# Gated cross-attention and a mixture of experts: token-major rows loaded first, one unbroken warming, and routing moved by one batch

## The chip, the cores and the metric

The kernel runs on one core of a Trainium2 chip. A core has a matmul engine (TensorE, PE in the profile), a vector engine (VectorE, DVE), an activation engine (ScalarE, ACT), a general engine (GpSimd, POOL) and a queue engine (SyncE, SP); each runs its own list of instructions in order, and they meet at semaphores. The metric is the device time of one execution in microseconds (us), lower is better.

## What is computed

Eight batches of 112 tokens with 256 values each, a context of 375 rows for each batch, and eight experts.

```python
def _L0_xattn_ref(x, w1, w2):                 # w1 = w2 = ctx_1024, one context per batch
    h = jnp.einsum('eth,efh->etf', x, w1)
    g = jax.nn.gelu(h, approximate=True)
    return jnp.einsum('etf,efh->eth', g, w2)

def _L0_ffn_ref(x, gate_w, gate_b, w1, b1, w2, b2):
    logits = xf @ gate_w.T + gate_b           # xf: all 896 tokens
    top1 = jnp.argmax(logits, axis=-1)
    ...
    h = jax.nn.relu(xf @ w1[e].T + b1[e])     # for each expert e of 8
    y = h @ w2[e].T + b2[e]
    out = out + jnp.where((top1 == e)[:, None], y, ...)

x = x + jnp.tanh(g_xattn[0]) * _L0_xattn_ref(_layernorm(x), ctx_1024, ctx_1024)
x = x + jnp.tanh(g_ffn[0]) * _L0_ffn_ref(_layernorm(x), gate_w, gate_b, w1, b1, w2, b2)
```

## The kernel before, in words

The program has two halves. The first is the attention, batch by batch (b = 0 to 7). The second sends each token only to its own expert: tokens are sorted into blocks of 128 rows by expert, gathered from DRAM, and each block passes through its expert.

**Loads.** SyncE issues all loads in one queue, in the order of its code (L237 to L261): the rows of batch 0 and of batch 1, the transposed contexts (`cxT`, 375 KB each) of batches 0 and 1, the rows of batches 2 and 3, those of 4 to 7, then the plain context rows (`cx`) and the other contexts, then weights. After the weights of expert 1 and the first half of expert 2 it waits until the gathered rows of the first blocks have landed (L255 to L258), and loads the rest.

**Attention.** For a batch, VectorE takes mean and variance (`stats_x`, L508 and L510), GpSimd makes 1/std (`of_x`, L305 and L308), VectorE normalises (`norm_x`, L514), TensorE transposes (`turn_xn`, L855) and ScalarE copies (`xnT_copy`, L414). TensorE then computes `scores` (L865) and the gate logits of x (`x_logits`, L874; VectorE scales them in L519), ScalarE applies gelu (L422), and TensorE applies `attend` (L883). VectorE adds the result to x (`add_attention`, L525), takes the statistics of the new rows (L532, L536), GpSimd makes their 1/std (`of_x2`), and ScalarE stores the rows to DRAM (`store_x2`, L430). TensorE runs `scores(b + 1)` ahead of `attend(b)`. Before the first rows are there it multiplies an identity matrix by itself (`keep_warm`, L962): 4, 4, 2 and 1 times, between other steps.

**Routing.** `route` on VectorE (L553 to L572) finds the expert of each token of a batch. `rank_sums` on TensorE (L890 to L899, small bf16 matmuls) counts the tokens of the same expert that stand before each token; `own_count` and `rank_of` (L600, L605), or `rank_one` (L609) for one batch, read the count out on VectorE. `pick` on GpSimd (L320) turns a rank into a 0/1 matrix. From the picks of batches 0 to 2 TensorE makes the first block of expert 0 without a gather (`first_block`, L920, after ScalarE's L436); from all of them it makes the table of rows (`tokens`, L926), for which it also needs `place` (L326). The order in which GpSimd takes these steps is written by hand:

```python
            for b in range(B - 1):
                of_x2(b)
                if b == 4:
                    for c in range(EARLY):
                        pick(c, 1)
            for b in range(3, 6):
                pick(b, 2)
            of_x2(B - 1)
            place()
            pick(6, 3)
```

**Experts.** TensorE runs `up` (L946; 32 matmul records for a block) and `down` (L955; 16 records), with `turn_block` (L933) between, for nine blocks; `up(0, (0,))` and `up(0, (1,))` are two eighths of the first, which stand among the rank sums. ScalarE and VectorE apply bias and relu (L464, L754), VectorE finishes a block (L770), GpSimd gathers blocks (L344) and scatters results (L349).

Of the kernel before, what the change touches and what calls it, by code (L numbers as in the profile page):

```python
# [19 lines left out]
P = 128  # L20
# [19 lines left out]
RAW = X0 + D  # L40
SL = S + E
CHUNKS = TOKENS // P
WARM = 4
AHEAD = 4
EARLY = 3
BLOCKS = E + 1
# [7 lines left out]
def gated_cross_attention_moe(nc, x, ctx, small, w1t, w2t, b2, out):  # L54
    x2_dram = nc.dram_tensor("x2_rows", (TOKENS, ROW), F32, kind="Internal").ap()
    with ExitStack() as stack:
# [6 lines left out]
        def sem(name):  # L63
            return stack.enter_context(nc.semaphore(name))
# [101 lines left out]
        y_over_ps = banks[7]  # L166

        def ranks(b):
            return {B - 2: banks[1], B - 1: banks[6]}.get(b, rk_ps)


        x_in = [sem("x_in0"), sem("x_in1"), sem("x_in2"), sem("x_in4")]
        small_in, b2_in = sem("small_in"), sem("b2_in")
        cxT_in = [sem("cxT_in0"), sem("cxT_in1"), sem("cxT_in2")]
        cx_in = [sem(f"cx_in{b}") for b in range(B)]
# [43 lines left out]
        @block.sync  # L219
        def _(sp):  # L220
            def load_context(b):
                sp.dma_start(cxs[:, b, :], ctx[b]).then_inc(cx_in[b], 16)

            def load_context_T(b):
                sp.dma_start(cxT[:, b, :], ctx[b, :, 0:KD * CTX]).then_inc(cxT_in[b], 16)

            def load_context_rows(b):
                sp.dma_start(cx[:, b, :], ctx[b, :, KD * CTX:CW]).then_inc(cx_in[b], 16)

            def load_expert(e):  # L230
                sp.dma_start(w1[:, e, :], w1t[e]).then_inc(w1_in[e], 16)
                sp.dma_start(w2[:, e, :], w2t[e]).then_inc(w2_in[e], 16)

            def load_x(b, n):
                return sp.dma_start(x2[0:S, b:b + n, X0:RAW], x[b * S:(b + n) * S].rearrange("(b p) d -> p b d", p=S))  # L235

            load_x(0, 1).then_inc(x_in[0], 16)  # L237
            load_x(1, 1).then_inc(x_in[1], 16)
            load_context_T(0)
            load_context_T(1)  # L240
            load_x(2, 2).then_inc(x_in[2], 16)
            load_x(4, 4).then_inc(x_in[3], 16)
            load_context_rows(0)
            load_context_T(2)
            load_context_rows(1)
            load_context_rows(2)
            for b in range(3, B):
                load_context(b)

            load_expert(0)  # L250
            sp.dma_start(b2b[:], b2.partition_broadcast(P)).then_inc(b2_in, 16)
            load_expert(1)
            sp.dma_start(w1[:, 2, :], w1t[2]).then_inc(w1_in[2], 16)

            sp.wait_ge(xnT_done, B)  # L255
            sp.wait_ge(xgT_done, 1)
            sp.wait_ge(first_in[1], 16)
            sp.wait_ge(xg_in[0], 16)  # L258
            sp.dma_start(w2[:, 2, :], w2t[2]).then_inc(w2_in[2], 16)
            for e in range(3, E):  # L260
                load_expert(e)  # L261

        @block.gpsimd
        def _(pool):
# [49 lines left out]
            def of_x2(b):  # L314
                pool.wait_ge(stats2_ok, b + 1)
                inverse_std(x2[0:S, b, MEAN:X0]).then_inc(rstd2_ok, 1)

            def pick(b, group):
                pool.wait_ge(rank_ok, group)
                pool.tensor_scalar(pick_r0[0:S, b, :], iota_r[0:S, :], rank[0:S, b:b + 1], None,  # L320
                                   ALU.is_equal).then_inc(picks0_ok, 1)
# [6 lines left out]

            for b in range(B):
                of_x(b)  # L330
            for b in range(B - 1):
                of_x2(b)
                if b == 4:
                    for c in range(EARLY):
                        pick(c, 1)
            for b in range(3, 6):
                pick(b, 2)
            of_x2(B - 1)
            place()
            pick(6, 3)  # L340


            def gather(to, idx):
                return pool.indirect_dma_start(  # L344
# [157 lines left out]
        @block.vector  # L502
        def _(dve):
            def stats_x(b):
                dve.wait_ge(x_in[b if b < 2 else 2 + b // 4], 16)
                if b >= 1:
                    dve.wait_ge(stats_ok, b)
                dve.bn_stats(stats[0:S, :], x2[0:S, b, X0:RAW]).then_inc(s1_ok, 1)  # L508
                dve.wait_ge(s1_ok, b + 1)
                dve.bn_aggr(mv[0:S, b, 0:2], stats[0:S, :]).then_inc(stats_ok, 1)  # L510

            def norm_x(b):
                dve.wait_ge(rstd_ok, b + 1)
                dve.tensor_scalar(xn[0:S, b, :], x2[0:S, b, X0:RAW], mv[0:S, b, 0:1], mv[0:S, b, 2:3],  # L514
                                  ALU.subtract, ALU.mult).then_inc(xn_ok, 1)

            def x_logits(b):
                dve.wait_ge(lg_done, b + 1)
# [78 lines left out]

            def own_count(b, n, group):
                dve.wait_ge(rk_done, group)
                dve.tensor_tensor(rk[0:S, b:b + n], rk_ps[0:S, b * E:(b + n) * E].rearrange("p (b e) -> p b e", b=n),  # L600
                                  oh[0:S, b:b + n], ALU.mult).then_inc(rank_read, 1)

            def rank_of(b, n, group):
                dve.wait_ge(rank_read, group)
                dve.tensor_reduce(rank[0:S, b:b + n], rk[0:S, b:b + n], AX_X, ALU.add).then_inc(rank_ok, 1)  # L605
# [10 lines left out]
                                  idw[0:S, B - 1, :].unsqueeze(2).to_broadcast([S, 2, E]), ALU.mult).then_inc(place_last_ok, 1)  # L616

            def pick_last():
                dve.wait_ge(rank_ok, 4)
                dve.tensor_scalar(pick_r0[0:S, B - 1, :], iota_r[0:S, :], rank[0:S, B - 1:B], None,  # L620
                                  ALU.is_equal).then_inc(pick_last_ok, 1)

            stats_x(0)
            stats_x(1)
            dve.wait_ge(gm_done, 1)
            for q in range(2):
                dve.tensor_tensor(xnT[:, q, :].rearrange("p (k n) -> p k n", k=KD)[:, :, S:SL],
                                  gw.rearrange("p (k e) -> p k e", k=KD),
                                  gm_ps[:, 0:E].unsqueeze(1).to_broadcast([P, KD, E]), ALU.subtract).then_inc(gwc_ok, 1)
            norm_x(0)  # L630
            norm_x(1)
            for b in range(2, 6):
                stats_x(b)
            norm_x(2)
            norm_x(3)
            dve.wait_ge(tg_ok, 1)
            dve.wait_ge(consts_ok, 11)
            x_logits(0)
            stats_x(6)
            stats_x(7)  # L640
            norm_x(4)
            norm_x(5)

            for b in range(B):
                add_attention(b)
                stats_x2(b)
                join_x2(b)
                if b + 1 < B:
                    x_logits(b + 1)
                if b == 0:  # L650
                    norm_x(6)
                    norm_x(7)
                if 1 <= b <= EARLY:
                    norm_x2(b - 1)
                if b == 3:
                    route(0, 3, 1)
                    is_expert_0()
                if b == 4:
                    skip_room()
                    own_count(0, 3, 1)  # L660
                    rank_of(0, 3, 1)
                    route(3, 1, 2)
                if b == 5:
                    route(4, 1, 3)
                if b == 6:
                    route(5, 1, 4)
            route(6, 1, 5)
            own_count(3, 3, 2)
            rank_of(3, 3, 2)
            route(7, 1, 6)  # L670
            place_last()
            rank_one(6, 3)
            rank_one(7, 4)
            pick_last()

            dve.wait_ge(tok0_done, 1)
# [172 lines left out]
        def _(pe):  # L849
# [58 lines left out]
                mm.then_inc(rk_done, 1)  # L908

            def rank_sums_before_last():  # L910
                for back in range(1, B):
                    batches_before(B - 1, 1, back, start=(back == 1), stop=False)
                past_room(B - 1, 1)
# [49 lines left out]

            pe.wait_ge(ident_ok, 1)
            keep_warm(WARM)
            pe.wait_ge(gmean_ok, 1)
            pe.wait_ge(small_in, 16)
            for k in range(KD):
                mm = pe.matmul(gm_ps[:, 0:E], g_mean[:], gw[:, k * E:(k + 1) * E], start=(k == 0), stop=(k == KD - 1))
            mm.then_inc(gm_done, 1)  # L970
            keep_warm(4)
            turn_xn(0)
            keep_warm(2)
            turn_xn(1)
            keep_warm(1)
            pe.wait_ge(gwc_ok, 2)
            scores(0)
            x_logits(0)
# [1 line left out]
            for b in range(B):  # L980
                if b + 1 < B:
                    scores(b + 1)
                    x_logits(b + 1)
                if b + 2 < B:
                    turn_xn(b + 2)
                attend(b)
                if b == 4:
                    pe.wait_ge(consts_ok, 11)
                    pe.wait_ge(oh_ok, 1)
                    for c in range(EARLY):  # L990
                        pe.matmul(rk_ps[0:1, B * E:(B + 1) * E], ones[0:S, 0:1], oh[0:S, c, :], start=(c == 0),
                                  stop=(c == EARLY - 1))
                    rank_sums(0, 3)

            for b in range(EARLY):
                pe.wait_ge(pick_x_ok, b + 1)
                mm = first_block(b)
            mm.then_inc(xgT_done, 1)
            pe.wait_ge(oh_ok, 4)
            rank_sums(3, 3)  # L1000
            up(0, (0,))
            pe.wait_ge(oh_ok, 5)
            rank_sums(6, 1)
# [136 lines left out]
```

## Time and profile before

| | us |
|---|---|
| median of 3 runs | 121.02 (119.59 to 121.82) |
| the profiled execution | 120.62 |
| its span | 118.8 |
| TensorE busy | 107.0 |
| VectorE busy | 54.5 |
| GpSimd busy | 37.4 |
| ScalarE busy | 27.2 |
| mean granted TensorE clock | 0.958 of full |

The span is the part of the execution between the first and the last instruction of the engines; the profiled execution took 1.8 us more than that. TensorE is busy for nine tenths of the span, so the stretches that matter are those in which it is idle or its granted clock is low. "Busy" says nothing of how fast the work goes: a matmul at half the clock is as busy as one at full clock.

### The profile page before, as it was taken

The page shows a single profiled execution, that of the slowest core. Times are in us where ns is not written, and L with a number is a line of the kernel's source. Part 1 is how long each engine was busy: PE and PEld are TensorE (multiplying, and loading weights), DVE is VectorE, ACT ScalarE, POOL GpSimd, SP SyncE. Part 2 cuts the span into 40 slices and gives each one's busy share as a digit, 9 for nine tenths or more (in the row PEclk, how much of TensorE's full clock was granted, in tenths as well). Part 3 has the DMA queues.
Part 4 walks back from the last instruction along what each step waited for, and adds up shares of the span by engine and source line. Part 5 has one row for each costly group of instructions (what it writes and reads, how often), then busy time and mean ns, then how long its engine had stood idle before and what let it go on. Part 6 is the DMA issues. An engine that isn't in the chain of part 4 may idle for free.

```text
span 118.8 us, 2178 instructions
## 1 busy us (share of the span) xinstructions
PE 107.0 (90%) x741; PEld 98.8 (83%) x742; DVE 54.5 (46%) x210; ACT 27.2 (23%) x82; POOL 37.4 (32%) x81
## 2 busy tenths in 40 slices
PE   4999999999968938999999999999999999999900
PEld 4999799997946928999999999989999899998800
DVE  0706965579666447566465351333422243141210
ACT  5521322220313120423332230412304123030000
POOL 6705742222522454770060273302003030030330
PEclk9999999999999995599999999999999999999995
DMA  3999999999999410359999999999401000010100
GB/s 91 241 271 302 417 415 413 420 428 405 429 419 423 186 39 3 77 126 390 368 417 416 372 419 378 399 425 430 197 19 40 0 0 34 0 44 0 37 18 28
DMA packets 7037, 28.32 MB, mean 238 GB/s; under 512 B 1133, under 2 KB 2927, under 8 KB 4848
## 3 DMA queue, kind: packets, MB, share of 16 engines
q1 hardware_dynamic: 4992, 25.06, 54.2%
q0 software_dynamic: 864, 2.12, 6.1%
q10 hardware_dynamic: 1168, 0.98, 2.5%
q8 instruction: 7, 0.11, 0.4%
q14 instruction: 6, 0.05, 0.1%
HBM read 26.30 MB, written 2.11 MB: 239 GB/s over the span
## 4 chain that ended last, share of the span: by engine, by line
PE 74%; DVE 8%; DMA 6%; POOL 4%; issue 2%; SPq 2%; POOLq 0%; DVEq 0%
PE bank L946 29%; PE bank L955 26%; PE bank L883 8%; DMA x<-in_x 6%; PE bank L865 6%; POOL pick_r L320 2%; PE bank L933 1%; PE bank L874 1%; DVE x L525 1%; DVE stats L532 1%; SPq L235 1%; DVE cand L563 1%; POOL out_rows L349 1%; PE bank L855 1%; DVE lg L553 1%
## 5 line engine op out<-in xcount | busy, mean ns | idle before, releaser
L946 PE MATMUL bank<-region,w 128*128 128x128 f32 x288 | 37.1, 289 | 0.0
L946 PEld LDWEIGHTS bank<-region,w 128*128 128x128 f32 x288 | 36.2, 203 | 0.5
L955 PE MATMUL bank<-w,region 128*128 128x256 f32 x144 | 32.6, 379 | 0.0
L955 PEld LDWEIGHTS bank<-w,region 128*128 128x128 f32 x144 | 26.7, 191 | 3.2
L464 ACT ACTIVATE region<-bank,smalls 128x128 f32<-128x128 f32 x40 | 12.5, 363 | 46.4 <-PE bank L946 42.8
L349 POOL DMA_INDIRECT out_rows<-region,to_row x9 | 8.9, 989 | 36.7 <-DVE region L770 36.1
L754 DVE TENSOR_SCALAR region<-bank,smalls 128x128 f32<-128x128 f32 x32 | 9.7, 346 | 16.0 <-PE bank L946 15.4
L344 POOL DMA_INDIRECT region<-x_rows,from_row x9 | 9.3, 1031 | 15.5 <-DMA region<-x_rows,from_row 12.0
L770 DVE SCALAR_TENSOR_TENSOR region<-bank,tg,region 128x256 f32<-128x256 f32 (+1 forms) x9 | 4.3, 483 | 20.9 <-PE bank L955 20.9
L883 PE MATMUL bank<-region,w 125*112 125x264 f32 x48 | 12.2, 389 | 1.7 <-DVE x L519 1.7
L865 PEld LDWEIGHTS bank<-xnT,region 128*125 128x125 f32 x96 | 12.4, 202 | 0.4
L865 PE MATMUL bank<-xnT,region 128*125 128x120 f32 x96 | 12.7, 286 | 0.0
L883 PEld LDWEIGHTS bank<-region,w 125*112 125x112 f32 x48 | 7.8, 176 | 3.8 <-issue 2.3
L422 ACT ACTIVATE w<-bank 125x336 f32<-125x336 f32 x8 | 3.6, 450 | 16.6 <-PE bank L865 13.5
L962 PE MATMUL bank<-ident 128*128 128x128 f32 x22 | 5.9, 437 | 1.6 <-POOL ident L268 1.6
L525 DVE SCALAR_TENSOR_TENSOR x<-bank,tg,x 112x264 f32<-112x264 f32 x8 | 3.9, 491 | 6.4 <-PE bank L883 6.4
L508 DVE BATCH_NORM_STATS2 stats<-x 112x6 f32<-112x256 f32 x8 | 3.4, 426 | 6.9 <-DMA x<-in_x 6.5
L962 PEld LDWEIGHTS bank<-ident 128*128 128x128 f32 x22 | 5.1, 331 | 1.3 <-POOL ident L268 1.3
L305 POOL TENSOR_TENSOR x<-x,eps 112x1 f32<-112x1 f32 x8 | 1.5, 190 | 13.7 <-DVE x L536 13.7
L320 POOL TENSOR_SCALAR pick_r<-iota_r,rank 112x128 bf16<-112x128 bf16 x7 | 4.2, 605 | 5.0 <-DVE rank L605 3.7
L308 POOL TENSOR_TENSOR mv<-mv,power 112x1 f32<-112x1 f32 x8 | 4.6, 574 | 0.6
L441 ACT ACTIVATE region<-bank 128x256 f32<-128x256 f32 x9 | 3.5, 384 | 5.6 <-PE bank L933 4.5
(117 smaller groups left out, 88.3 us busy)
## 6 DMA issues: line engine op xcount, KB each, us to landing
w<-in_w1t SPq DMA_DIRECT2D x8, 1024.0 KB, 22.0
w<-in_w2t SPq DMA_DIRECT2D x8, 1024.0 KB, 22.2
region<-in_ctx SPq DMA_DIRECT2D x5, 771.0 KB, 13.5
region<-in_ctx SPq DMA_DIRECT2D x3, 396.0 KB, 9.0
region<-in_ctx SPq DMA_DIRECT2D x3, 375.0 KB, 5.7
b2b<-in_b SPq DMA_DIRECT2D x1, 1024.0 KB, 24.5
x_rows<-x ACTq DMA_DIRECT2D x8, 113.8 KB, 6.6
x<-in_x SPq DMA_DIRECT2D x1, 448.0 KB, 7.7
```

Of the source, the lines that this page charges most:

```text
L308: return pool.tensor_tensor(v[:, 2:3], v[:, 3:4], power[0:S, :], ALU.pow)
L320: pool.tensor_scalar(pick_r0[0:S, b, :], iota_r[0:S, :], rank[0:S, b:b + 1], None, ALU.is_equal).then_inc(picks0_ok, 1)
L344: return pool.indirect_dma_start(out=to, out_offset=None, in_=x2_dram, in_offset=bass.IndirectOffsetOnAxis(ap=idx, axis=0), bounds_check=T ...
L349: return pool.indirect_dma_start(out=out, out_offset=bass.IndirectOffsetOnAxis(ap=idx, axis=0), in_=rows, in_offset=None, bounds_check=TOK ...
L464: act.activation(hidT[:, q, 2 * k + r, :], hT_ps[k][:, r * P:(r + 1) * P], ACT.Relu, bias=b1[:, bass.ds(e * KH + 2 * k + r, 1)]).then_inc( ...
L525: dve.scalar_tensor_tensor(out=x2[0:S, b, X0:ROW + E], in0=at_ps[b % 2][0:S, 0:DL], scalar=tg[0:S, 0:1], in1=x2[0:S, b, X0:ROW + E], op0=A ...
L754: dve.tensor_scalar(hidT[:, q, 2 * k + r, :], hT_ps[k][:, r * P:(r + 1) * P], b1[:, bass.ds(e * KH + 2 * k + r, 1)], 0.0, ALU.add, ALU.max ...
L865: mm = pe.matmul(sc_ps[b % 2][0:CR, c * SL:(c + 1) * SL], cxT[:, b, k * CTX + c * CR:k * CTX + (c + 1) * CR], xnT[:, b % 2, k * SL:(k + 1) ...
L883: mm = pe.matmul(at_ps[b % 2][0:S, 0:DL], gel[0:CR, b % 2, c * S:(c + 1) * S], cx[0:CR, b, c * DL:(c + 1) * DL], start=(c == 0), stop=(c = ...
L946: mm = pe.matmul(hT_ps[k][:, part % 2 * P:(part % 2 + 1) * P], w1[:, e, n * H + part * P:n * H + (part + 1) * P], xgT[:, j % 2, n * P:(n + ...
L955: mm = pe.matmul(y[:, 0:D], hidT[:, q, part, :], w2[:, e, part * D:(part + 1) * D], start=(part == 0), stop=(part == KH - 1))
L962: pe.matmul(sc_ps[1][:, 0:P], ident[:], ident[:], start=True, stop=True)
```

## The change

Five things change. (1) x is given to the program with the token first, `(S, B, D)`, and the rows of batches 2 to 7 are one load of 6 KB for each partition, issued ahead of the contexts. (2) The warming of TensorE is nine multiplications in one stretch ahead of the first transpose, and one more ahead of the second. (3) VectorE's first steps come in another order: the rows of batches 0 and 1 are normalised before the gate weights are centred, and the statistics and normalisations of batches 5, 6 and 7 are all done before the first `add_attention`. (4) The routing steps after batch 4 move one batch later or earlier: ranks of batches 0 to 2 are read in step 5 and no longer in step 4, those of 3 and 4 form a group that is summed and read in step 6, and batch 5 is taken alone right after the loop; the sums of 3 and 4 go to another PSUM bank. (5) On GpSimd, picks are issued behind the 1/std of a later batch: 0 to 2 behind that of batch 5, 3 and 4 behind that of batch 6, and the 1/std of batch 7 no longer stands behind the pick of batch 5.

```diff
-WARM = 4
+WARM = 9
...
-            return {B - 2: banks[1], B - 1: banks[6]}.get(b, rk_ps)
+            return {EARLY: banks[6], B - 2: banks[1], B - 1: banks[6]}.get(b, rk_ps)
...
-                return sp.dma_start(x2[0:S, b:b + n, X0:RAW], x[b * S:(b + n) * S].rearrange("(b p) d -> p b d", p=S))
+                return sp.dma_start(x2[0:S, b:b + n, X0:RAW], x[:, b:b + n, :])
             load_x(0, 1).then_inc(x_in[0], 16)
             load_x(1, 1).then_inc(x_in[1], 16)
+            load_x(2, B - 2).then_inc(x_in[2], 16)
             load_context_T(0)
             load_context_T(1)
-            load_x(2, 2).then_inc(x_in[2], 16)
-            load_x(4, 4).then_inc(x_in[3], 16)
...
-            for b in range(B - 1):
+            for b in range(6):
                 of_x2(b)
-                if b == 4:
-                    for c in range(EARLY):
-                        pick(c, 1)
-            for b in range(3, 6):
+            for b in range(EARLY):
+                pick(b, 1)
+            of_x2(6)
+            for b in range(EARLY, 5):
                 pick(b, 2)
-            of_x2(B - 1)
+            of_x2(7)
+            pick(5, 3)
             place()
-            pick(6, 3)
+            pick(6, 4)
...
+            def centre_gates(q):
+                dve.wait_ge(gm_done, 1)
+                dve.tensor_tensor(xnT[:, q, :].rearrange("p (k n) -> p k n", k=KD)[:, :, S:SL],
+                                  gw.rearrange("p (k e) -> p k e", k=KD),
+                                  gm_ps[:, 0:E].unsqueeze(1).to_broadcast([P, KD, E]), ALU.subtract).then_inc(gwc_ok, 1)
...
             stats_x(0)
             stats_x(1)
-            dve.wait_ge(gm_done, 1)
-            for q in range(2):
...
             norm_x(0)
             norm_x(1)
-            for b in range(2, 6):
-                stats_x(b)
+            centre_gates(0)
+            centre_gates(1)
+            stats_x(2)
+            stats_x(3)
             norm_x(2)
+            stats_x(4)
             norm_x(3)
             dve.wait_ge(tg_ok, 1)
             dve.wait_ge(consts_ok, 11)
             x_logits(0)
-            stats_x(6)
-            stats_x(7)
-            norm_x(4)
-            norm_x(5)
+            for b in range(5, B):
+                stats_x(b)
+                norm_x(b - 1)
+            norm_x(B - 1)
...
-                if b == 0:
-                    norm_x(6)
-                    norm_x(7)
...
                 if b == 4:
+                    route(3, 1, 2)
+                if b == 5:
+                    route(4, 1, 3)
                     skip_room()
                     own_count(0, 3, 1)
                     rank_of(0, 3, 1)
-                    route(3, 1, 2)
-                if b == 5:
-                    route(4, 1, 3)
                 if b == 6:
                     route(5, 1, 4)
+                    own_count(3, 2, 2)
+                    rank_of(3, 2, 2)
+            rank_one(5, 3)
             route(6, 1, 5)
-            own_count(3, 3, 2)
-            rank_of(3, 3, 2)
             route(7, 1, 6)
             place_last()
-            rank_one(6, 3)
-            rank_one(7, 4)
+            rank_one(6, 4)
+            rank_one(7, 5)
             pick_last()
...
             def rank_sums_before_last():
+                pe.wait_ge(rank_read, 2)
...
             keep_warm(WARM)
+            turn_xn(0)
             pe.wait_ge(gmean_ok, 1)
             pe.wait_ge(small_in, 16)
...
-            keep_warm(4)
-            turn_xn(0)
-            keep_warm(2)
+            keep_warm(1)
             turn_xn(1)
-            keep_warm(1)
             pe.wait_ge(gwc_ok, 2)
...
+                if b == 6:
+                    pe.wait_ge(oh_ok, 3)
+                    rank_sums(3, 2)
+            pe.wait_ge(oh_ok, 4)
+            pe.wait_ge(rank_read, 1)
+            rank_sums(5, 1)
             for b in range(EARLY):
                 pe.wait_ge(pick_x_ok, b + 1)
                 mm = first_block(b)
             mm.then_inc(xgT_done, 1)
-            pe.wait_ge(oh_ok, 4)
-            rank_sums(3, 3)
             up(0, (0,))
             pe.wait_ge(oh_ok, 5)
             rank_sums(6, 1)
```

## Rows read from the trace of the kernel before

**Rows 1.** The page, parts 1 and 2: TensorE's share, its granted clock in 40 slices

```profile
PE 107.0 (90%) x741; PEld 98.8 (83%) x742; DVE 54.5 (46%) x210; ACT 27.2 (23%) x82; POOL 37.4 (32%) x81
...
PEclk9999999999999995599999999999999999999995
```

**Rows 2.** Busy time by stretch: PE, PEld, DVE, ACT, POOL, clock, DMA share, GB/s

```profile
42.00:44.00 2.00, 0.13 (x2) 0.00 (x0) 0.94 (x5) 0.62 (x2) 1.15 (x4) 1.00 0.10 29
44.00:46.00 2.00, 1.40 (x27) 1.28 (x28) 1.25 (x12) 0.00 (x0) 0.62 (x1) 0.52 0.10 33
...
51.00:54.00 3.00, 3.00 (x18) 2.62 (x17) 2.60 (x15) 0.65 (x3) 1.89 (x2) 1.00 0.68 192
```

**Rows 3.** The chain that ended last, 40 to 63 us: start, length, what

```profile
40.32 1.77 POOL pick_r L320 x3
...
42.32 0.58 POOL x L308
42.92 0.34 DVE lg L553
...
45.80 5.33 PE bank L946 x24
...
54.80 2.68 PE bank L946 x24
...
62.76 0.22 PE bank L933 x2
```

**Rows 4.** The timeline, 34 to 45 us: start, length, engine, line, idle before

```profile
34.69 0.49 DVE L525 SCALAR_TENSOR_TENSOR x<-bank,tg,x 112x264 f32<-112x264 f32 x1 [0.76 <-PE bank L883]
...
36.18 1.56 PE L883 MATMUL bank<-region,w 125*112 125x264 f32 x6 [1.53 <-DVE x L519]
...
37.20 0.98 ACT L436 ACTIVATE w<-pick_r,is_e 112x128 f32<-112x128 bf16 x3 [3.77 <-POOL x L308]
37.65 1.60 PE L920 MATMUL bank<-w 112*128 112x128 f32 x12
...
38.77 0.18 DVE L536 BATCH_NORM_AGGREGATE x<-stats 112x2 f32<-112x6 f32 x1
...
40.52 0.83 PE L894 MATMUL bank<-oh,ones 112*112 112x8 bf16 x13
...
41.42 0.71 PE L946 MATMUL bank<-region,w 128*128 128x128 f32 x4
...
44.16 0.25 PE L890 MATMUL bank<-oh,tri 112*112 112x8 bf16 x1 [2.03 <-DVE oh L572]
```

**Rows 5.** The timeline, 1 to 19 us

```profile
1.60 2.07 PE L962 MATMUL bank<-ident 128*128 128x128 f32 x8 [1.60 <-POOL ident L268]
...
8.23 2.30 PE L865 MATMUL bank<-xnT,region 128*125 128x120 f32 x12
...
10.87 0.43 DVE L508 BATCH_NORM_STATS2 stats<-x 112x6 f32<-112x256 f32 x1 [0.68 <-DMA x<-in_x]
...
14.29 0.70 DVE L514 TENSOR_SCALAR w<-x,mv 112x256 f32<-112x256 f32 x2
14.91 0.49 DVE L525 SCALAR_TENSOR_TENSOR x<-bank,tg,x 112x264 f32<-112x264 f32 x1
...
17.82 1.47 PE L865 MATMUL bank<-xnT,region 128*125 128x120 f32 x12
```

**Rows 6.** Issues in short windows, 2.6 to 4 us: KB each, us to landing

```profile
x<-in_x SPq DMA_DIRECT2D x1, 224.0 KB, 6.1
...
x<-in_x SPq DMA_DIRECT2D x1, 448.0 KB, 7.7
region<-in_ctx SPq DMA_DIRECT2D x1, 396.0 KB, 8.2
```

**Rows 7.** The timeline at 51 us, and that gather's time to landing

```profile
50.89 1.00 POOL L344 DMA_INDIRECT region<-x_rows,from_row  x1 [0.30 <-issue]
...
region<-x_rows,from_row POOLq DMA_INDIRECT x1, 8.2
```

More of the change, by code:

```diff
@@ L168, in ranks @@
         def ranks(b):
-            return {B - 2: banks[1], B - 1: banks[6]}.get(b, rk_ps)
-        x_in = [sem("x_in0"), sem("x_in1"), sem("x_in2"), sem("x_in4")]
+            return {EARLY: banks[6], B - 2: banks[1], B - 1: banks[6]}.get(b, rk_ps)
+        x_in = [sem("x_in0"), sem("x_in1"), sem("x_in2")]
         small_in, b2_in = sem("small_in"), sem("b2_in")
@@ L504, in stats_x @@
             def stats_x(b):
-                dve.wait_ge(x_in[b if b < 2 else 2 + b // 4], 16)
+                dve.wait_ge(x_in[min(b, 2)], 16)
                 if b >= 1:
@@ L599, in own_count @@
                 dve.wait_ge(rk_done, group)
-                dve.tensor_tensor(rk[0:S, b:b + n], rk_ps[0:S, b * E:(b + n) * E].rearrange("p (b e) -> p b e", b=n),
+                dve.tensor_tensor(rk[0:S, b:b + n], ranks(b)[0:S, b * E:(b + n) * E].rearrange("p (b e) -> p b e", b=n),
                                   oh[0:S, b:b + n], ALU.mult).then_inc(rank_read, 1)
@@ L618, in pick_last @@
             def pick_last():
-                dve.wait_ge(rank_ok, 4)
+                dve.wait_ge(rank_ok, 5)
                 dve.tensor_scalar(pick_r0[0:S, B - 1, :], iota_r[0:S, :], rank[0:S, B - 1:B], None,
@@ L624, in _ @@
             stats_x(1)
-            dve.wait_ge(gm_done, 1)
-            for q in range(2):
-                dve.tensor_tensor(xnT[:, q, :].rearrange("p (k n) -> p k n", k=KD)[:, :, S:SL],
-                                  gw.rearrange("p (k e) -> p k e", k=KD),
-                                  gm_ps[:, 0:E].unsqueeze(1).to_broadcast([P, KD, E]), ALU.subtract).then_inc(gwc_ok, 1)
             norm_x(0)
             norm_x(1)
-            for b in range(2, 6):
-                stats_x(b)
+            centre_gates(0)
+            centre_gates(1)
+            stats_x(2)
+            stats_x(3)
             norm_x(2)
+            stats_x(4)
             norm_x(3)
@@ L1116 @@
     arrays = {
-        "x": np.ascontiguousarray(x).reshape(TOKENS, D),
+        "x": np.ascontiguousarray(np.asarray(x).transpose(1, 0, 2)),
         "ctx": np.ascontiguousarray(np.concatenate([
```

## The prediction

> **What bounds the kernel now.** I read the page's slices first. TensorE is busy nine tenths of the span, and two slices at 45 to 51 us carry a granted clock of 5 tenths [rows 1]. So I asked for busy time by stretch around those slices. From 42 to 44 us TensorE does 0.13 us of work, from 44 on its clock is 0.52, and it is back at 1.00 from 51 us [rows 2]. These levels are 2.4 and 1.2 GHz. From 51 us to the end the chain of waits is TensorE alone, but for one last block's finish and scatter: whatever makes the expert phase start earlier or run faster there is worth its full length, and nothing else is.
>
> The chain names what holds TensorE at 42 to 45 us [rows 3]: three picks on GpSimd (1.77 us from 40.32), behind them the 1/std of batch 7 (0.58 from 42.32), then VectorE's route of batch 7 (from 42.92), then one more pick, then 24 matmuls of `up(0)` that take 5.33 us. The same 24 take 2.68 us at 54.80 [rows 3]. The statistics of batch 7 were ready at 38.77 + 0.18 = 38.95 [rows 4]; its 1/std stood 3.1 us behind picks which themselves waited for rank sums. That is the queue that part (5) of the change rearranges.
>
> **The change, part by part. First the routing.** I put the new order on the times of before, with the durations of before.
>
> GpSimd: the picks of 0 to 2 (1.77 us) leave 29.89 and go behind the 1/std of batch 5. VectorE reads their ranks in step 5, after `route(4)`. Those five instructions (L590 to L605) take 0.9 us, 0.18 each like L536 [rows 4]; in step 5 VectorE had 0.76 us idle ahead of its L525 at 34.69 [rows 4], so step 6 starts some 0.14 us later, and so does `attend(7)`, which waits for step 6's L519: 36.32 and not 36.18, its end 37.85. In step 4 the same 0.9 us goes away, where nothing waited for it. The picks now run from 34.85 to 36.62. The 1/std of batch 6 stands behind them: statistics ready at 36.0, start at 36.65 instead of 35.94, done 37.45. ScalarE is queued behind that with the store of batch 6 and then L436, which began at 37.20 [rows 4]; now 37.9. So `first_block` starts at 38.35 instead of 37.65 and ends at 39.95 instead of 39.25. This is a cost of 0.7 us on TensorE's path. Its cover is `rank_sums(5, 1)`, 7 small matmuls of some 0.08 us (13 took 0.83 us with their overlap [rows 4], 16 with a change of weights 1.25), which TensorE does in the gap, 37.9 to 38.5. `rank_sums(3, 2)`, 6 of them, goes into the 1.53 us for which TensorE waits ahead of `attend(7)` [rows 4]: it needs L593's result, done at 34.4, before TensorE is free at 34.65. Both together replace `rank_sums(3, 3)`, which stood on the path from 39.25 to 39.73. The new wait for `rank_read` 2 costs nothing: that read is done at 37.4, four us ahead.
>
> From 39.95 TensorE's path is: ScalarE's copy and first eighth 39.95 to 40.9 (before 39.25 to 40.17 with rank sums between; an eighth is 4 records, each 2.68/24 = 0.11 [rows 3]); 16 small matmuls for batches 6 and 7, 1.25 us, to 42.15; the second eighth (41.42 in before [rows 4]) to 42.6. The one-hot of batch 6 that the 16 wait for: VectorE ends batch 7's statistics at 39.05, reads the rank of 5 (0.3) and routes 6 (1.06; the route of 7 took 42.92 to 44.16 [rows 3, 4]): 40.4, in time.
>
> Batch 7: `pick` 3 and 4 run on GpSimd from 37.56 (rank read in step 6) to 38.75, before batch 7's statistics at 39.08. So its 1/std is done at 39.95, where before it was 42.9. VectorE starts `route(7)` when it is done with `route(6)`, at 40.4, and ends by 41.6, where before TensorE met the one-hot at 44.16 after a 2.03 us stall [rows 4]. Pick of 5 and `place` fit between 39.95 and 41. The rank of 6 is summed at 41.55, read by 42.0, and its pick (1.77/3 = 0.59 [rows 3]) done by 42.7. TensorE's last sum is at 42.7, rank of 7 read 42.95, VectorE's pick 43.25, last `tokens` 43.4, the 9 counting matmuls 43.75. The remaining 24 matmuls of `up(0)` start at 43.8 instead of 45.80: **2.0 us won**.
>
> **The clock.** Before, TensorE had two idle gaps (2.03 us and 0.44 us) between 42 and 45.2 us. In the order above it has none over 0.5 us from 37.85 on. If the clock then stays at 2.4 GHz the 24 matmuls take 2.68 us and not 5.33 [rows 3]: **2.65 us won**. Sum at the start of the `down(0)`: 46.5 instead of 51.13, 4.65 us.
>
> **Does it last to the end?** What is late next are the gathers. The first follows the table by 1.2 us and its rows were normalised 4.7 us after the last `tokens`: 48.2, and TensorE wants them at 49.05. The fourth gather (block 3) was issued at 50.89 and took 8.2 us [rows 7], because SyncE's 11 MB of weights are let go at 51.3 and share the engines with it. All of this moves 2.0 us forward only, to 57.05 and, normalised, 57.5. TensorE turned block 3 at 62.5 [rows 3]; minus 4.65 this is 57.8. Slack 0.3 us, and VectorE's 3.9 us of `over_picks` leave 0.5 us for the relu that `up(2)` needs. I count both as hidden; if that fails it costs what is missing, up to the whole 2.65 minus slack. Later blocks have 5 us and more. The weights of expert 3 and on came two us or more ahead of their use and stay so by the same shift.
>
> **The start.** SyncE's queue completes in order. In KB up to each: before, rows 2 and 3 are at 1198 and landed at 2.65 + 6.1 = 8.75 (issue and time to landing); rows 4 to 7 at 1646 and 3.12 + 7.7 = 10.8; `cx(0)` at 2042 and 3.63 + 8.2 = 11.8 [rows 6]. In the new order `cxT(0)` is at 1271, where it was at 599. Between the first two that is 8.75 + 73/448 x 2.05 = 9.1, so `scores(0)` starts at 9.1, where before it was 8.23 [rows 5]; that the larger pieces make it as early as 8.0, or nothing before 9.8, are the bounds. The clock in exchange: 8 records of warming took 2.07 us, 12 of `scores(0)` 2.30 us, 12 of a later batch 1.47 us [rows 5], so before, TensorE was at the lower level to about 10 us. Nine warmings are 18 records, 4.65 us: unbroken from 1.60 to 6.2. If that lifts the clock before 9 us, `scores(0)` takes 1.47 us and the first logits are there at 10.9, else at 11.7. VectorE is then the bound: from there it does three statistics (0.43 [rows 5] and the 0.18 behind, 0.74 from one to the next), four normalisations (0.70/2 [rows 5]) and a wait of 0.5 for the last 1/std before L525 of batch 0, 4.15 us with the gaps: 15.15, or 15.9, against 14.91 [rows 5]. `attend(1)` followed L525 by 1.57 us with 0.3 us to spare, so the start costs between 0 and +0.7; with the context at 8.0 and a high clock it would win 0.8. I take 0. All transfers having arrived, the 3.19 us pitch of the batches is TensorE's own and stays.
>
> The Trainium skill ("DMA: Bandwidth & Descriptors", section "Anatomy of one DMA — SWDGE (gpsimd) path") gives a DMA about 2.0 us plus its bytes at 436 GB/s, for GpSimd's own issues. By it 1271 KB from 0.81 us on would be there at 5.8 us (an estimate from that page), and `scores(0)` would not be held at all. The trace doesn't agree: the 1646 KB up to the last rows took 10.0 us where the formula has 5.9. The sum above goes by the trace.
>
> **Sum.** 118.8 - 2.0 - 2.65 + 0 = 114.15 us of span. With the 1.8 us around it: 116.0 us, against the profiled 120.62, which is 0.4 below the median of 121.02. I predict 116.0.
>
> **Rivals.**
> (a) *The clock falls all the same.* For it: from 39.95 to 43.8 TensorE has only two eighths and some 40 tiny matmuls, and it fell 2 us into a gap that followed just such work. Against it: the long gap is gone, and around 35 us it had a gap of 1.53 us and kept its clock [rows 1, 4]. Then 2.65 us are not won, or only partly: 118.8 - 2.0 + 1.8 = 118.6, from 117.6 to 119.4. 22%.
> (b) *The gathers become the bound.* The clock is high but block 3 lands as late as before or VectorE's `over_picks` hold `up(2)`: 1 to 2 us of the 4.65 are lost, 117.3. For it: a slack of 0.3 us. Against it: nothing in the chain lengthens. 10%.
> (c) *Slower: contexts behind the rows, at the low clock.* TensorE has nothing to do from some 6.8 us to 9.1 us, waiting for `cxT(0)`. If that gap undoes the warming, scores and attends of the first batches run at 1.2 GHz, where a batch costs 6.4 us and not 3.19. Eight us of such work cost 8 us more than at full clock, less the 0.8 that before lost at this place: 116.0 + 7.2 = 123.2. It outweighs the gain from 4.65 + 0.8 us of such work on. Against it: before, the clock rose at 10 us after a start with shorter gaps and stayed. 6%.
> (d) *It doesn't do what it says:* `route(7)` is not earlier because GpSimd's picks of 3 and 4 wait for ranks read late. Then only the start changes: 120.5. 3%.
>
> **How the numbers follow.** The forecast has 59%, its own range 115.0 to 117.3 (start from -0.8 to +0.7, rest of the routing path +-0.5). The range over cases with 8 in 10: 114.8 to 119.0. A difference of 2% (2.4 us, to 118.6) is about what a measurement tells from none. Faster: all of the forecast and of (b), and four tenths of (a): 0.78. Same: the rest of (a), (d), and a part of (c): 0.16. Slower: 0.06.
>
> **What would show it.** Right: no slice at 5 tenths in the middle of the span; TensorE's wait for L572 gone; GpSimd's L308 of batch 7 at about 39.4; 24 L946 matmuls in 2.7 us beginning near 43.8; `turn_block` of block 3 near 57.8 with no stall. The start right: L865 first at 8.5 to 9.5, and L525 first at about 15. Wrong: a low clock in either place, an idle PE at 57 us named to L748, or first scores held past 10 us.

## The result: 119.12 us at the median against 120.18, and a spread of 5 us

| | median us | lowest to highest | runs |
|---|---|---|---|
| before | 120.18 | 119.46 to 121.82 | 12 |
| changed | 119.12 | 116.03 to 121.43 | 12 |

The ratio is 0.9736 (95% interval 0.9673 to 0.9798). It is formed from the runs within 1.5% of each kernel's fastest, and of the changed kernel that leaves out most runs; by the medians it is 119.12/120.18 = 0.991, which at 2% is no difference. The figure that matters is the second column: three of the twelve runs are at 116.0 to 117.2, near the 116.0 that was forecast, and six at 119.5 to 121.4, within the range of before. The profiled execution, 120.44 us with a span of 118.6, is one of the latter, and it shows why.

The page's slices of the changed kernel, to be held against [rows 1]:

```profile
PE 107.3 (90%) x745; PEld 98.3 (83%) x746; DVE 54.6 (46%) x212; ACT 27.1 (23%) x82; POOL 37.7 (32%) x81
...
PEclk9985559999999999999999999999999999999997
```

The low clock at 45 to 51 us is gone, and another stands at 8 to 18 us. Busy time by stretch of the changed kernel (columns as in [rows 2]):

```profile
5.40:6.90 1.50, 1.46 (x10) 1.06 (x10) 0.57 (x3) 0.36 (x1) 0.55 (x1) 1.00 1.09 280
6.90:8.50 1.60, 0.00 (x0) 0.00 (x0) 0.64 (x3) 0.36 (x1) 0.05 (x1) 0.89 1.02 382
8.50:12.00 3.50, 3.46 (x17) 3.49 (x18) 1.81 (x6) 0.53 (x2) 2.27 (x6) 0.50 1.04 397
...
15.50:18.40 2.90, 2.90 (x10) 2.14 (x9) 0.43 (x2) 0.36 (x1) 0.39 (x1) 0.50 1.03 423
...
42.00:44.00 2.00, 1.60 (x12) 1.41 (x12) 1.79 (x11) 0.89 (x3) 1.53 (x4) 1.00 0.20 55
44.00:46.00 2.00, 1.93 (x22) 1.80 (x23) 1.14 (x7) 0.02 (x1) 0.83 (x3) 1.00 0.21 62
```

TensorE does nothing from 6.9 to 8.5 us, and then works 10 us at half its clock. The timeline says what it waits for (compare [rows 5]):

```profile
1.60 3.75 PE L964 MATMUL bank<-ident 128*128 128x128 f32 x18 [1.60 <-POOL ident L267]
...
6.48 0.41 PE L856 MATMUL bank<-ident,w 112*128 112x112 f32 x2
...
8.54 2.85 PE L866 MATMUL bank<-xnT,region 128*125 128x120 f32 x12 [1.65 <-DMA region<-in_ctx]
...
15.49 2.85 PE L884 MATMUL bank<-region,w 125*112 125x264 f32 x6
...
18.38 0.49 DVE L530 SCALAR_TENSOR_TENSOR x<-bank,tg,x 112x264 f32<-112x264 f32 x1 [2.05 <-PE bank L884]
```

The 18 warming records took 3.75 us where 8 took 2.07 before, so the clock rose during them, some 5 us earlier than before by these durations. Up to 6.9 us the records are at full pace, and right behind the wait for the transposed context, 1.65 us, they are at half pace: the 12 records of `scores(0)` take 2.85 us and not 1.47. The first L530 comes at 18.38 instead of 14.91 [rows 5]. The issue rows of the changed kernel (compare [rows 6]):

```profile
x<-in_x SPq DMA_DIRECT2D x1, 672.0 KB, 6.0
region<-in_ctx SPq DMA_DIRECT2D x1, 375.0 KB, 6.2
```

They were issued at 1.71 and 2.17, so rows 2 to 7 land at 7.7 and `cxT(0)` at 8.4. The routing stretch did what was forecast (timeline; compare [rows 4]):

```profile
39.82 1.56 PE L884 MATMUL bank<-region,w 125*112 125x264 f32 x6 [1.08 <-DVE x L524]
...
41.54 0.98 ACT L435 ACTIVATE w<-pick_r,is_e 112x128 f32<-112x128 bf16 x3 [4.47 <-POOL x L307]
...
41.99 1.41 PEld L922 LDWEIGHTS bank<-w 112*128 112x128 f32 x12 [0.21 <-ACT w L435]
...
42.67 0.19 POOL L304 TENSOR_TENSOR x<-x,eps 112x1 f32<-112x1 f32 x1 [0.39 <-DVE x L541]
...
44.07 0.71 PE L948 MATMUL bank<-region,w 128*128 128x128 f32 x4 [0.47 <-ACT region L440]
```

and in the chain that ended last (compare [rows 3]):

```profile
38.48 1.79 POOL pick_r L319 x3
...
47.58 2.88 PE bank L948 x24
50.45 2.59 PE bank L957 x12
53.05 0.24 issue
...
62.55 0.22 PE bank L935 x2
```

From the start of `attend(7)` to the 24 matmuls: 47.58 - 39.82 = 7.76 us, before 45.80 - 36.18 = 9.62. From there to the end of the span: 118.6 - 47.58 = 71.0, before 118.8 - 45.8 = 73.0. The 24 matmuls themselves are shorter by 2.45 us; the rest, 0.47, goes at block 1 (the 0.24 at 53.05, and an L935 of 0.44 where before it took 0.22). The routing won 1.86 us of stall and 2.0 us of clock; the start, with `attend(7)` at 39.82 instead of 36.18, took 3.64 back. That closes the sum: -0.2 us of span.

### The profile page after: what moved, and what is told of

It reads as the page before. It is cut to its first block, busy times and chain, and to the rows that moved or that the text cites. A ratio compares the mean times of both kernels' runs of the same rounds, so it can differ in the third digit from the quotient of the medians.

```text
span 118.6 us, 2188 instructions
## 1 busy us (share of the span) xinstructions
PE 107.3 (90%) x745; PEld 98.3 (83%) x746; DVE 54.6 (46%) x212; ACT 27.1 (23%) x82; POOL 37.7 (32%) x81
## 4 chain that ended last, share of the span: by engine, by line
PE 78%; DVE 6%; DMA 5%; POOL 3%; issue 2%; SPq 1%; ACT 1%; ACTq 0%; POOLq 0%; DVEq 0%
PE bank L948 28%; PE bank L957 26%; PE bank L866 9%; PE bank L884 7%; DMA region<-in_ctx 5%; PE bank L875 2%; PE bank L935 2%; POOL pick_r L319 2%; PE bank L922 1%; PE bank L856 1%; SPq L235 1%; DVE x L530 1%; POOL out_rows L348 1%; DVE stats L537 1%; PE bank L895 1%
## 5 line engine op out<-in xcount | busy, mean ns | idle before, releaser
L948 PE MATMUL bank<-region,w 128*128 128x128 f32 x288 | 34.6, 277 | 0.5 <-ACT region L440 0.5
L948 PEld LDWEIGHTS bank<-region,w 128*128 128x128 f32 x288 | 33.7, 192 | 1.1 <-ACT region L440 0.7
L866 PEld LDWEIGHTS bank<-xnT,region 128*125 128x125 f32 x96 | 14.2, 227 | 2.4 <-issue 1.8
L866 PE MATMUL bank<-xnT,region 128*125 128x120 f32 x96 | 14.7, 313 | 1.6 <-DMA region<-in_ctx 1.6
L884 PE MATMUL bank<-region,w 125*112 125x264 f32 x48 | 13.5, 421 | 1.1 <-DVE x L524 1.1
L884 PEld LDWEIGHTS bank<-region,w 125*112 125x112 f32 x48 | 8.6, 193 | 3.0 <-issue 1.1
L530 DVE SCALAR_TENSOR_TENSOR x<-bank,tg,x 112x264 f32<-112x264 f32 x8 | 3.9, 492 | 9.1 <-PE bank L884 9.1
L964 PE MATMUL bank<-ident 128*128 128x128 f32 x20 | 4.2, 387 | 1.6 <-POOL ident L267 1.6
L964 PEld LDWEIGHTS bank<-ident 128*128 128x128 f32 x20 | 3.9, 293 | 1.3 <-POOL ident L267 1.3
```

Of the source, the lines that this page charges most:

```text
L530: dve.scalar_tensor_tensor(out=x2[0:S, b, X0:ROW + E], in0=at_ps[b % 2][0:S, 0:DL], scalar=tg[0:S, 0:1], in1=x2[0:S, b, X0:ROW + E], op0=A ...
L866: mm = pe.matmul(sc_ps[b % 2][0:CR, c * SL:(c + 1) * SL], cxT[:, b, k * CTX + c * CR:k * CTX + (c + 1) * CR], xnT[:, b % 2, k * SL:(k + 1) ...
L884: mm = pe.matmul(at_ps[b % 2][0:S, 0:DL], gel[0:CR, b % 2, c * S:(c + 1) * S], cx[0:CR, b, c * DL:(c + 1) * DL], start=(c == 0), stop=(c = ...
L948: mm = pe.matmul(hT_ps[k][:, part % 2 * P:(part % 2 + 1) * P], w1[:, e, n * H + part * P:n * H + (part + 1) * P], xgT[:, j % 2, n * P:(n + ...
L964: pe.matmul(sc_ps[1][:, 0:P], ident[:], ident[:], start=True, stop=True)
```

## The experiments

In each, 6 runs of the kernel stand beside 11 of the kernel before on the same chip. Medians of before were 120.51, 120.23 and 120.04 us in the three sets (first: routing alone to held clock; second: contexts first to eighths; third: the rest).

**The two halves of the change, apart.** The first kernel is before with parts (4) and (5), the second is before with (1), (2) and (3); the edits are those of the diff.

> The kernel before with the routing parts alone (4 and 5); loads, warming and VectorE's first steps are those of before. Theory (the routing gives 4.3 us by 2.0 us of stall and 2.3 to 2.65 us of clock, the new start gives part of it back): 115.8 to 116.8 us, steady from run to run like before, the 24 matmuls of up(0) at full clock. Rival (the routing gives only the stall, since the clock falls there in many runs): 117.5 to 119. Rival (the new start is what makes the good runs of the change fast): no better than 118.

> The kernel before with the start parts alone (1, 2 and 3: token-major rows ahead of the contexts, nine warmings in a row, VectorE's first steps); the routing is that of before. Theory (the start costs 0 to 5 us, by whether TensorE's clock falls in its wait for the first context): 120 to 125 us, spread over 3 us or more, median 122.5. Rival (the start is harmless and the spread of the changed kernel comes from its routing): 119.5 to 121, spread below 1.5 us.

Routing alone: 117.16 us (116.09 to 117.72), ratio 0.9735 (0.9659 to 0.981). Start alone: 123.01 us (120.67 to 123.56), ratio 1.0241 (1.0165 to 1.0318). The routing is worth 3.3 us at the median, the start costs 2.5, and the two make the changed kernel's 1.1. That the good runs need the new start fell: the changed kernel has its best at 116.0, the routing alone at 116.1. The timeline of the start alone, from its fastest run (120.67):

```profile
6.73 0.42 PE L855 MATMUL bank<-ident,w 112*128 112x112 f32 x2
8.56 2.16 PE L865 MATMUL bank<-xnT,region 128*125 128x120 f32 x12 [1.42 <-DMA region<-in_ctx]
```

The same wait, then half clock from 9.3 to 12.6 us, a part of `scores(0)` and of `scores(1)`. The five other runs are at 121.8 to 123.6 and have no trace. But routing alone stayed above the expected 115.8 to 116.8. Its busy time by stretch and its timeline:

```profile
42.00:43.00 1.00, 0.76 (x27) 0.65 (x24) 0.55 (x5) 0.62 (x2) 0.00 (x0) 1.00 0.00 0
43.00:44.00 1.00, 1.00 (x7) 0.98 (x6) 0.93 (x10) 0.00 (x0) 0.00 (x0) 0.52 0.00 0
...
46.00:47.00 1.00, 1.00 (x9) 1.00 (x8) 0.25 (x3) 0.24 (x1) 0.70 (x2) 0.77 0.59 150
```

```profile
39.64 0.71 PE L948 MATMUL bank<-region,w 128*128 128x128 f32 x4 [0.47 <-ACT region L441]
...
43.08 4.54 PE L948 MATMUL bank<-region,w 128*128 128x128 f32 x24
```

So the clock falls at 43 us with no idle stretch over half a microsecond behind `attend(7)`, as rival (a) had it, for about half as long as before: 4.54 us for the 24 matmuls, not 5.33 and not 2.88.

**The gap filled.** The changed kernel with

```diff
             turn_xn(1)
+            keep_warm(6)
             pe.wait_ge(gwc_ok, 2)
             scores(0)
```

> The changed kernel with six more identity multiplications behind the second transpose, ahead of scores(0), so that TensorE is busy while it waits for the first context. Theory (the idle 1.6 us there let the clock fall): 115.8 to 117 us in nearly all runs, spread below 1.5 us, the profile without a low clock between 7 and 18 us. Rival (the clock falls at the start for another reason, such as too little warming in all): still 116 to 121, median near 119. Rival (the fillers themselves delay scores(0) where the clock is low): up to 2 us above the changed kernel.

117.56 us (116.55 to 120.9), ratio 0.9762 (0.9675 to 0.9848). Its timeline:

```profile
6.89 1.52 PE L964 MATMUL bank<-ident 128*128 128x128 f32 x12
8.25 1.47 PE L866 MATMUL bank<-xnT,region 128*125 128x120 f32 x12
...
43.26 4.57 PE L948 MATMUL bank<-region,w 128*128 128x128 f32 x24
```

With the gap filled by work `scores(0)` runs at full clock, and four of six runs are at 116.5 to 117.7. The expected level was missed all the same: only one run is below 117, since this kernel, too, loses the clock in the routing (24 matmuls in 4.57 us), where the changed kernel's profile did not. The other two runs were 118.64 and 120.9; of those there is no trace. That the fillers themselves ran at a low clock in them is possible and not shown.

**The clock alone.** The kernel before with

```diff
             up(0, (1,))
+            keep_warm(9)
             pe.wait_ge(oh_ok, 6)
```

> The kernel before with nine identity multiplications in TensorE's idle stretch at 42 to 44 us (between the second eighth of up(0) and the last rank sum), nothing else. Theory (of the 4.65 us some 2.65 are the clock alone): the 24 matmuls take 2.7 us, the stall stays, 120.2 - 2.4 = 117.8 us. Rival (the clock falls there whatever stands in the gap, because of the small matmuls): 120.2 unchanged.

117.85 us (117.51 to 118.15), ratio 0.9817 (0.976 to 0.9875). Timeline:

```profile
41.42 2.17 PE L962 MATMUL bank<-ident 128*128 128x128 f32 x18
43.62 0.21 PE L890 MATMUL bank<-oh,tri 112*112 112x8 bf16 x1
...
45.16 2.94 PE L946 MATMUL bank<-region,w 128*128 128x128 f32 x24
```

Nothing of the order changed, the last pick comes 8.3 us after the start of `attend(7)` as before, and 2.7 us are gone at the median. Of the 3.3 us that the routing parts give, 2.7 can thus be had by keeping TensorE busy. The spread is 0.6 us, where before had 4.3 on the same chip: its three runs above 122 have a mean granted clock of 0.929 to 0.943, the others 0.956 to 0.969, so they are runs with more low clock, too.

**Which part of the start.** Each of the next four is the changed kernel with one part undone. First the order of the loads:

```diff
-            load_x(2, B - 2).then_inc(x_in[2], 16)
             load_context_T(0)
             load_context_T(1)
+            load_x(2, 2).then_inc(x_in[2], 16)
+            load_x(4, 4).then_inc(x_in[3], 16)
...
```

> The changed kernel with the old order of its loads: the rows of batches 2 and 3 and of 4 to 7 (two loads) behind the first two transposed contexts; all else as changed, the token-major layout too. Theory (rows ahead of the contexts delay the first context to 8.4 us and so open the 1.6 us gap in which the clock falls): cxT(0) lands near 6.3 us, the gap ahead of scores(0) is gone, scores(0) starts near 7 us, 116 to 117.5 us in nearly all runs, spread below 1.7 us. Rival (the changed warming is at fault by itself): median 118.5 to 119.5, spread 3 us or more.

117.94 us (117.26 to 118.20), ratio 0.9809 (0.9759 to 0.9859). Timeline:

```profile
7.06 0.36 PE L857 MATMUL bank<-ident,w 112*128 112x112 f32 x2
7.25 1.53 PE L867 MATMUL bank<-xnT,region 128*125 128x120 f32 x12
...
13.52 1.57 PE L867 MATMUL bank<-xnT,region 128*125 128x120 f32 x12 [0.56 <-ACT xnT L414]
15.74 0.56 PE L876 MATMUL bank<-xnT 128*112 128x8 f32 x4 [0.65 <-DVE x L531]
...
44.14 4.57 PE L949 MATMUL bank<-region,w 128*128 128x128 f32 x24
```

The gap and the spread are gone with the load order, as the theory had it: none of six above 118.2. The level was missed: two of six are within 116 to 117.5, the median is 0.4 above it. With the rows late, VectorE's new order (all statistics and normalisations ahead of the first `add_attention`) makes TensorE wait at 15 us; the wait at 13 us is for ScalarE's copy L414, which had stood behind L425's wait for context rows. `attend(7)` begins at 36.45, with the routing alone at 35.38, and the two profiled executions differ by the same 1.1 us (118.20 and 117.14). The clock falls in the routing here as well.

The warming:

```diff
-WARM = 9
+WARM = 4
...
             keep_warm(WARM)
-            turn_xn(0)
...
-            keep_warm(1)
+            keep_warm(4)
+            turn_xn(0)
+            keep_warm(2)
             turn_xn(1)
+            keep_warm(1)
```

> The changed kernel with the warming of before (4, 4, 2 and 1 multiplications between the steps), loads and VectorE order as changed. Theory (the gap ahead of scores(0) stays about as long, so the warming can't help): the clock is low for scores(0) and scores(1) in most runs, median 118 to 120 us, like the changed kernel's 119.1. Rival (one unbroken warming is what makes the clock fall again, since it ends too early): median 117.2 as in the kernel with the routing parts alone.

118.35 us (116.7 to 119.16), ratio 0.9815 (0.9739 to 0.9891). Here the theory was wrong in its first half. The trace:

```profile
7.73 0.66 PE L964 MATMUL bank<-ident 128*128 128x128 f32 x2
8.40 1.93 PE L866 MATMUL bank<-xnT,region 128*125 128x120 f32 x12
```

There is no gap to speak of: at half clock the old warming and transposes last until 8.4 us, just as long as `cxT(0)` takes. By these rows a clock that rises early makes the work ahead of the gap shorter and the gap longer. At the median the old warming is 0.8 us below the changed kernel, and its highest run 2.3 us below that one's; with such spreads this is an indication. The median lies within the expected 118 to 120; two of the six, at 119.0 and 119.2, have a mean granted clock of 0.96, so the loss is rarer or smaller and not gone.

VectorE's normalisations of batches 6 and 7:

```diff
             for b in range(5, B):
                 stats_x(b)
-                norm_x(b - 1)
-            norm_x(B - 1)
+            norm_x(4)
+            norm_x(5)
...
+                if b == 0:
+                    norm_x(6)
+                    norm_x(7)
```

> The changed kernel with the normalisations of batches 6 and 7 back behind the first add_attention; statistics of 5 to 7 stay ahead of it. Theory (the first add_attention of a run whose clock stays high waits for VectorE, some 1.2 us of work and a wait for 1/std): the best runs gain 0.4 to 0.8 us (115.3 to 115.7 instead of 116.0), the median stays near 119 because the clock decides it. Rival (TensorE or the contexts are the bound there): best runs 116.0 as before.

119.96 us (115.44 to 120.17): four of six at 119.9 to 120.2, the best one 0.6 us under the changed kernel's best. Both are as expected and fit VectorE as the bound of a good run. But the gain is read from one run of six against one of twelve, and neither has a trace, so it is not shown.

The layout of x:

```diff
-                return sp.dma_start(x2[0:S, b:b + n, X0:RAW], x[:, b:b + n, :])
+                return sp.dma_start(x2[0:S, b:b + n, X0:RAW], x[b * S:(b + n) * S].rearrange("(b p) d -> p b d", p=S))
```

> The changed kernel with x laid out batch-major again, all else as changed (rows of 2 to 7 still one load ahead of the contexts). Theory (the layout does little: the rows went in pieces of 1 KB before, and the order of the loads is what counts): rows of 2 to 7 land within 0.5 us of the changed kernel's 7.7, median 118.5 to 120, same spread. Rival (6 KB runs of a row in DRAM speed that load up): rows and first context land 0.7 us or more later, median above 120.

119.84 us (117.8 to 121.56). Issue row and timeline:

```profile
x<-in_x SPq DMA_DIRECT2D x1, 672.0 KB, 6.5
```

```profile
9.13 2.85 PE L866 MATMUL bank<-xnT,region 128*125 128x120 f32 x12 [2.38 <-DMA region<-in_ctx]
```

Rows 0.5 us later, `scores(0)` 0.6 us later and the gap 2.38 us. The same load laid out token-major landed 5.5 to 6.1 us after its issue in six traces of this study, against 6.5 in this one trace: the layout seems worth 0.4 us or more of landing when the rows stand ahead of the contexts. At the median this is 0.7 us above the changed kernel, with spreads of 4 and 5 us, so no difference in time is shown.

**Better versions.** In the kernel with the routing parts alone, two eighths of `up(0)` at each of the two places among the rank sums:

```diff
-            up(0, (0,))
+            up(0, (0, 1))
...
-            up(0, (1,))
+            up(0, (2, 3))
...
-            up(0, range(2, KH))
+            up(0, range(4, KH))
```

> The kernel before with the routing parts alone, and two eighths of up(0) instead of one at each of the two places among the rank sums (same work, other order). The kernel with the routing parts alone lost the clock for 3.4 us at 43 us. Theory (what TensorE does from 39 to 43 us, small matmuls and waits, lets it fall; larger ones among them hold it): the clock stays high, 115.5 to 116.3 us in all runs. Rival (the clock falls all the same): 117.2. Rival (the later table of tokens, by 0.9 us, makes gathers late): 117 or more with a high clock and TensorE waiting for block 1 or block 3.

115.94 us (115.69 to 117.67), ratio 0.9658 (0.9608 to 0.9708). Timeline:

```profile
39.66 1.16 PE L948 MATMUL bank<-region,w 128*128 128x128 f32 x8 [0.47 <-ACT region L441]
...
41.79 1.16 PE L948 MATMUL bank<-region,w 128*128 128x128 f32 x8
...
43.99 2.05 PE L948 MATMUL bank<-region,w 128*128 128x128 f32 x16
```

In this profile the same matmuls in another order hold the clock (16 records in 2.05 us), and the median is 1.2 us below that of the routing alone (0.9 when each is taken against before on its own chip). One run, 117.67 at a mean granted clock of 0.972, is where the routing alone is. The table of tokens is 0.9 us later and TensorE waited for no gather. With x token-major and the old load order besides:

> The kernel with the routing parts and the eighths, on the old start, and x laid out token-major with the old loads in the old order. Theory (layout alone moves nothing on the path): 115.7 to 116.5 us, median within 0.5 us of 115.9. Rival (it helps the rows of 4 to 7 land earlier, for which VectorE waited at 10.9 us in the kernel before): attend(0) 0.5 us earlier and 115.4.

116.07 us (115.55 to 117.71), ratio 0.9699 (0.9631 to 0.9766): no difference, as expected; two of its six runs, at 117.4 and 117.7, have a mean granted clock of 0.972. And the changed kernel with three mends (filled gap, late norms, eighths):

> The changed kernel with three mends: six identity multiplications in the gap ahead of scores(0), the normalisations of 6 and 7 behind the first add_attention, two eighths of up(0) at each place among the rank sums. Theory (each removes what its own run showed): best runs 114.5 to 115.2 us, median 115 to 116. Rival (where the clock rises late the fillers delay scores(0)): a tail to 118 or more, median above the 115.9 of the kernel with the routing parts and eighths.

115.64 us (115.27 to 116.91), ratio 0.9698 (0.9631 to 0.9765). Timeline:

```profile
8.31 1.54 PE L869 MATMUL bank<-xnT,region 128*125 128x120 f32 x12
...
15.13 1.50 PE L887 MATMUL bank<-region,w 125*112 125x264 f32 x6
...
43.43 3.60 PE L951 MATMUL bank<-region,w 128*128 128x128 f32 x16
```

`attend(1)` is at 15.13; in the profile of before it is at 16.48, with the old start and eighths at 15.70, so here the new start wins half a microsecond or more. Yet the best run misses the expected 114.5 to 115.2 by a little. And this profile (116.53) loses the clock in spite of the eighths: 16 records in 3.60 us, not 2.05. So the eighths make the loss rarer and do not end it. Over the three kernels that have them, five of 18 runs have a mean granted clock of 0.971 to 0.973 and are at least 0.8 us above all others of their kernel; of the routing alone four of six are a microsecond above its best two. All mended and the old start with eighths are the two best kernels of the study, and 0.3 us between them is less than their spreads.

## Why the prediction was right, and where it was not

*The routing, 2.0 us of stall.* Right: 1.86 measured. The step at `attend(7)`, the later `first_block` behind GpSimd's picks (a wait of 0.21 us for L435), the rank sums in TensorE's idle stretch (its wait 1.08 instead of 1.53) and an early `of_x2(7)` are all in the rows. `of_x2(7)` begins at 42.67, 2.85 us after the start of `attend(7)`; before, its second half alone began 42.32 - 36.18 = 6.14 us after it [rows 3, 4].

*The clock, 2.65 us.* The mechanism is right: with the old order and the clock held the gain is 2.7 us. The size is luck of a run. The profile of the changed kernel has a full clock there, 24 matmuls in 2.88 us, and 2.0 us came of it; that of the routing alone has it low from 43.0 to 46.5 us, and they take 4.54. Of the seven profiles with the new routing and single eighths, four lose the clock there (routing alone, filled gap, contexts first, old warming: 4.29 to 4.57 us), and the three that keep it (changed, late norms, batch-major) are those that had run at half clock up to 18 us. Why is open; no run separates the two. The chance of rival (a), 22%, was too small: the argument that no idle stretch over half a microsecond remained didn't protect the clock.

*The gathers.* Block 3 did not hold TensorE, block 1 did, for 0.24 us (the "issue" piece at 53.05): the normalisation of its rows began 5.5 us after the last `tokens`, where before it began 4.3 us after. Why this gather landed later is open. Small, and inside what was counted.

*The start, 0 us.* This is the step that failed. Its landings were estimated at 9.1 us and came at 8.4, the good side. The gap was in the text too, as rival (c), from 6.8 us on. What failed was the judgement that a gap of this size leaves the clock alone, taken from the shorter gaps of before. By the prediction's own signs, a low clock in either place and L525 first at about 15, it was wrong here: the clock was 0.50 and L530 came at 18.38. The runs show a cost of 2.5 us at the median (start alone) and 3.64 us in the profiled execution. Rival (c) had the mechanism, but as one case of 7 us with 6%, where it is a common case of 3 to 4 us.

How far the gap alone does it: with a gap of 1.42 to 2.38 us ahead of `scores(0)` (changed, start alone, batch-major) the clock is low behind it in three profiles of three, and with the gap filled or gone (filled gap, all mended, contexts first) `scores(0)` takes 1.47 to 1.54 us in three of three. But in the profile of late norms the gap is 0.55 us, and the records ahead of it are at half pace already (two of warming in 0.77 us, where the changed kernel has 0.47). So a gap is enough here, and something else can cost the clock as well; what, no run shows.

So "faster" holds by the ratio (0.9736 of 121.02 is 117.8), which rests on the few runs that lost little clock, and that it comes near the forecast is luck in part. 116.0 is the best run (mean granted clock 0.993) and not the usual one, and the median of 119.12 lies 0.1 us above the range of 114.8 to 119.0. In terms of the prediction's parts it was -3.9 and +3.6 in the profiled execution, not -4.65 and 0.

The formula of the Trainium skill ("DMA: Bandwidth & Descriptors", section "Anatomy of one DMA — SWDGE (gpsimd) path"), made for GpSimd's own issues and weighed in the prediction, put `cxT(0)` at 5.8 us, an estimate. It landed at 8.4, so the trace again doesn't agree.

## What to carry to other kernels

Here a clock that had been raised early was lost again in a gap: before making TensorE faster ahead of a transfer, look when the transfer lands, and put the transfer that the next matmul needs ahead of those that VectorE needs later. Where TensorE has only small matmuls and short waits, spread large ones that must be done anyway among them; this was worth about a microsecond at the median here, by fewer runs that lost the clock, and it cost nothing that the traces show. When a kernel's times spread by 4%, look for a clock that some runs lose, and judge an edit by all of its runs, since one profile shows one of the cases.

## What the runs showed of the hardware

A wait of 1.65 us after 5 us of work was followed by 10 us at the lower level (0.50 in every stretch from 8.5 to 18.4 us), though TensorE was busy for nearly all of them. In the start alone a wait of 1.42 us was followed by 3.3 us of it. In the kernel before, a wait of 1.53 us at 35 us left the clock high, so the length of a wait doesn't settle it. The profile's clock column is no guide to the first microseconds: before, it reads 1.00 from 0 to 8 us while 8 records of 128x128 took 2.07 us, the half-clock pace. In the kernel with late norms it reads 1.00 all through the start, and 12 records of `scores(0)` take 2.84 us, behind a wait of 0.55 us and warming that is at half pace again:

```profile
PEclk9999999999999999999999999999999999999997
```

```profile
6.71 0.77 PE L967 MATMUL bank<-ident 128*128 128x128 f32 x2
...
8.40 2.84 PE L869 MATMUL bank<-xnT,region 128*125 128x120 f32 x12 [0.55 <-DMA region<-in_ctx]
```

The durations of like matmuls are the better witness there. The mean granted clock inherits that: this execution has 0.994 and took 120.09 us. A load of 672 KB whose rows stand together in DRAM landed 6.0 us after its issue (5.5 to 6.1 in six traces), the same bytes in 1 KB rows 6.5 (one trace).
